# A two-layer graph kernel: the product with the values one slot later, with four buffers for the probabilities

## The chip, the cores and the metric

The kernel runs on one core of a Trainium2 chip. The metric is the device time of one execution in microseconds (us). A core has four engines that compute, each with its own instruction stream: TensorE (PE in the profile, with its weight loads shown apart as PEld), VectorE (DVE), ScalarE (ACT) and GpSimd (POOL). SyncE (SP) only starts DMAs here. The streams meet only through semaphores, and each engine runs its instructions in order.

## The reference

Two graph layers over 4096 nodes with a 4096 x 4096 adjacency matrix, each followed by a residual sum and a layer norm:

```
mask = adj > 0
agg  = mask @ x / max(rowsum(mask), 1)
h    = relu(concat(x @ W_self + b_self, agg @ W_nb + b_nb) @ W_comb + b_comb)
x    = layernorm(x + h)                                   # layer 0
xa   = tanh(x @ Wx1 + bx1) @ Wx2 + bx2                    # 32 wide
na   = tanh(neigh @ Wn1 + bn1) @ Wn2 + bn2
ws   = softmax(where(adj > 0, leaky_relu(xa @ na.T), -9e15))
out  = layernorm(x + concat(x @ Wfx + bfx, ws @ (neigh @ Wv + bv)))   # layer 1
```

## The kernel before

The rows of x are worked on in 32 blocks of 128. A block's 4096 columns are taken in 8 groups of 512, k = 0 to 7. All engines walk through the same list of slots; `due(s, AT, k)` says whether in slot s an engine has the work whose offset is AT: block b, group g where s - AT = 8b + g. Work written with k = 0 comes once in a block, in the slots that have the same remainder modulo 8; below, "remainder 0" means those slots. The number of a slot is an order and not a clock: an engine goes on to the next slot as soon as its semaphores let it.

A preparation makes fp16 pairs (high and low half) of x and of the neighbours' values, and the 32-wide attention vectors of the neighbours. `neigh_sb` holds the neighbours' rows for that; it is not read any more once the preparation is over. Then the blocks follow. In each slot:

- TensorE: `turn_p` (line 951, four transposes of exponentials into one of two banks `ps_t`), `aggregate` (lines 927 and 930, eight matmuls of the mask with x), once in a block some small steps of layer 0 and 1, then `scores` (line 942), and last `weigh_values` (line 964, twelve matmuls of the probabilities' halves with the values into `ps_v`).
- ScalarE: `exps` in every other slot (line 761), `p_high` (line 767, the high half of the probabilities from `ps_t`), `leaky` (line 754, scores out of `ps_s`). Once in a block `mean_of` (744), the copies 749 and 785, `x_tanh` (790), `xatt_high` (796), `normalise1` (773) and `normalise2` (779).
- VectorE: `masked_scores` (line 572, score plus bias, and a maximum), `make_mask` in every other slot (line 480), `p_low` last (line 618, the low half: `ps_t` minus the high half). Once in a block `row_scale` (624 to 628), `layer1` (636 to 642), `degrees` (587 and 590), `layer0` (596 to 603), `row_max`, and 608 and 613.
- GpSimd: `make_bias` in every other slot (line 408), `norm1`, `norm2` (398 to 402) and `add_biases` (393).
- SyncE: the transposing DMAs of the mask, the loads of adj, and once in a block a load of x and a store.

Transposes of group k are made in slot 30 + 8b + k and its product with the values, before the change, in slot 31 + 8b + k, behind the aggregation and the scores of that slot. `weigh_values` waits for `p_low` of its own group; `turn_p` of group k waits for `p_low` of group k - 2, since there are two banks; `p_high` of group k waits until the product of group k - 2 is done, since there are two buffers of halves. `layer1` reads `ps_v` when the block's last product is done, and the next block's first product waits for that.

In slots of remainder 0, `degrees` of a block is what `mean_of` waits for on ScalarE. Two slots later ScalarE makes `x_tanh` (line 790), and TensorE's `x_attention` (line 1008) waits for it behind the aggregation of its slot.

Of the kernel before, what the change touches and what calls it, by code (L numbers as in the profile page):

```python
# [5 lines left out]
F32, F16, BF16, F8 = mybir.dt.float32, mybir.dt.float16, mybir.dt.bfloat16, mybir.dt.float8e4  # L6
# [6 lines left out]
P = 128  # L13
N = 4096
D = 256
H = 32
DV = 128
# [6 lines left out]
NG = N // GW  # L24
# [14 lines left out]
NT = NB // TR  # L39
BIAS_BUFS = 3  # L40
RES_BUFS = 4

# [13 lines left out]
SCORE_AT = 20  # L58
ROW_MAX_AT = 28
TURN_AT = 30  # L60
WEIGH_AT = 31
LAYER1_AT = 39
SLOTS = NG * (NB - 1) + LAYER1_AT + 1


# [18 lines left out]
def at_least(eng, sem, value):  # L84
    if value > 0:
        eng.wait_ge(sem, value)


def gnn_kernel(nc, x, adj, w_self, b_self, w_nb, b_nb, w_comb, b_comb, neigh, wx1, bx1, wx2, bx2,
# [5 lines left out]
    with ExitStack() as ctx:  # L95
        def sb(name, shape, dt):
            return ctx.enter_context(nc.sbuf_tensor(name, shape, dt))

        def sem(name):
            return ctx.enter_context(nc.semaphore(name))  # L100

        x16 = sb("x16", [P, NC, XW], F16)
        neigh_sb = sb("neigh_sb", [P, NB, D], F32)
        m_both = sb("m_both", [P, DC, 2 * D], F32)
        v16 = sb("v16", [P, NC, 2 * DV], F16)
# [22 lines left out]
        mask_t8 = mask_t[:, :, :, :].rearrange("p a c n -> p (a c n)").bitcast(F8).rearrange(  # L128
            "p (a c n e) -> p a c e n", a=2, c=NC // 2, e=2)
        score = sb("score", [P, 2, N], F32)  # L130
        late = sb("late", [P, 2048], F32)
        p_both = late[:, 0:1024].bitcast(F16).rearrange("p (a b n) -> p a b n", a=2, b=2)
        p_hi, p_lo = p_both[:, 0], p_both[:, 1]
        res = late[:, 1024:2048].rearrange("p (r d) -> p r d", r=RES_BUFS)
        x_in = sb("x_in", [P, 2, D], F32)
        l0 = sb("l0", [P, D], F32)
        mean = sb("mean", [P, D], F32)
# [43 lines left out]
        ps_t = [ctx.enter_context(nc.psum_tensor(f"ps_t{k}", [P, GW], F32)) for k in range(2)]  # L181
        ps_v = ctx.enter_context(nc.psum_tensor("ps_v", [P, GW], F32))
# [53 lines left out]
        pv_done = sem("pv_done")  # L236
# [21 lines left out]
        p_hi_made = sem("p_hi_made")  # L258
# [99 lines left out]
        def _(pool):  # L358
# [31 lines left out]
            def add_biases(b):  # L390
                pool.wait_ge(x1_made, b + 1)
                at_least(pool, out_made, b - RES_BUFS + 1)
                pool.tensor_tensor(res[:, b % RES_BUFS, :], x1[:, :], bfv_sb[:, :], ALU.add).then_inc(resx_made, 1)  # L393

# [33 lines left out]
        def _(dve):  # L428
# [182 lines left out]
            def add_fx(b):  # L611
                dve.wait_ge(resx_made, b + 1)
                dve.tensor_tensor(res[:, b % RES_BUFS, 0:DV], ps_x[:, 3 * P:4 * P], res[:, b % RES_BUFS, 0:DV],
                                  ALU.add).then_inc(res_made, 1)

            def p_low(b, k):
                dve.wait_ge(p_hi_made, NG * b + k + 1)
                dve.tensor_tensor(p_lo[:, k % 2, :], ps_t[k % 2][:, :], p_hi[:, k % 2, :],  # L618
                                  ALU.subtract).then_inc(p_lo_made, 1)

            def row_scale(b):
# [46 lines left out]
        def _(act):  # L668
# [94 lines left out]

            def p_high(b, k):
                act.wait_ge(pt_done, NG * b + k + 1)
                at_least(act, pv_done, NG * b + k - 1)
                act.copy(p_hi[:, k % 2, :], ps_t[k % 2][:, :]).then_inc(p_hi_made, 1)  # L767

            def normalise1(b):
                act.wait_ge(norm1_step, 3 * (b + 1))  # L770
# [53 lines left out]
        def _(pe):  # L824
# [129 lines left out]
            def weigh_values(b, k):  # L954
                pe.wait_ge(p_lo_made, NG * b + k + 1)
                if k == 0:
                    at_least(pe, l1_step, 6 * (b - 1) + 4)
                    if b == 0:
                        pe.wait_ge(h_tanh, NT)
                for u in range(CG):  # L960
                    c = k * CG + u
                    chunk = slice(u * P, (u + 1) * P)
                    for part, (p, v) in enumerate(((p_hi, 0), (p_hi, DV), (p_lo, 0))):
                        mm = pe.matmul(ps_v[:, 0:DV], p[:, k % 2, chunk], v16[:, c, v:v + DV],  # L964
                                       start=(c == 0 and part == 0), stop=(c == NC - 1 and part == 2))
                mm.then_inc(pv_done, 1)

# [85 lines left out]
```

## Time and profile before

| what | value |
|---|---|
| median of 3 runs | 807.25 us (806.93 to 810.67) |
| the profiled execution | 808.58 us, of which span 806.8 us |
| PE busy | 766.1 us, 95% |
| DVE busy | 593.4 us, 74% |
| ACT busy | 560.9 us, 70% |
| POOL busy | 293.9 us, 36% |
| granted TensorE clock, mean | 0.981 |

The span is the time from the first to the last instruction. The first 100 us are the preparation and the first block, the loop runs to about 750 us, where the last block's aggregation ends, and the rest is the tail, in which only layer 1 of the last blocks is left. A "wait" in the profile is idle time of an engine just before an instruction, put down to what released it.

### The profile page before, as it was taken

What the parts mean: (1) busy time and instruction counts of PE and PEld (TensorE: products, weight loads), DVE (VectorE), ACT (ScalarE), POOL (GpSimd) and SP (SyncE); (2) the same over time, 40 slices, a digit from 0 to 9 for tenths busy, and PEclk for the clock granted to TensorE, in tenths of its full rate; (3) what the DMA queues carried; (4) which work ended last, traced back from release to release, by engine and by line L of the source; (5) the groups of instructions that cost most, each with busy time, mean ns of one, the idle gap of its engine ahead of it and who ended that gap; (6) DMA issues with size and microseconds to landing.
All of it is one profiled execution on the core that took longest, in us unless ns stands there. A gap on an engine that the chain in (4) does not pass through costs nothing.

```text
span 806.8 us, 20198 instructions
## 1 busy us (share of the span) xinstructions
PE 766.1 (95%) x7440; PEld 643.2 (80%) x7440; DVE 593.4 (74%) x1481; ACT 560.9 (70%) x1045; POOL 293.9 (36%) x368
## 2 busy tenths in 40 slices
PE   5679989999999999999999999999999999999885
PEld 4446666888888888888888888888888888888664
DVE  2667456878777777877877777777778777777784
ACT  2246236777777777787777777777777777777995
POOL 0004163443333334444444333333444444443101
PEclk9679999999999999999999999999999999999999
DMA  7905574445454554554445444455544544420000
GB/s 237 364 21 157 140 200 138 136 122 138 141 120 135 145 144 123 135 145 125 132 139 135 129 138 131 126 138 145 127 136 139 145 123 134 139 66 15 14 9 14
DMA packets 107403, 103.64 MB, mean 128 GB/s; under 512 B 74664, under 2 KB 88872, under 8 KB 107304
## 3 DMA queue, kind: packets, MB, share of 16 engines
q1 hardware_dynamic: 105872, 101.29, 45.1%
q8 instruction: 59, 0.97, 0.5%
q10 hardware_dynamic: 1432, 1.06, 0.4%
q14 instruction: 40, 0.33, 0.1%
HBM read 81.34 MB, written 4.19 MB: 106 GB/s over the span
## 4 chain that ended last, share of the span: by engine, by line
PE 87%; DVE 5%; ACT 2%; issue 2%; SPq 2%; DMA 1%; POOL 1%; POOLq 0%; ACTq 0%; DVEq 0%
PE ps_v L964 20%; PE ps_agg L930 13%; PE ps_agg L927 13%; PE ps_t L951 13%; PE ps_agg L982 7%; PE ps_s L942 7%; PE ps_x L1002 2%; PE ps_x L999 2%; SPq L328 2%; PE ps_x L1008 2%; PE ps_s L843 1%; PE ps_v L851 1%; PE ps_x L860 1%; DMA neigh_sb<-in_L_gnn_neigh_dram 1%; PE ps_agg L972 1%
## 5 line engine op out<-in xcount | busy, mean ns | idle before, releaser
L754 ACT ACTIVATE score<-ps_s,sc 128x512 f32<-128x512 f32 x256 | 177.8, 695 | 93.4 <-PE ps_s L942 89.5
L927 PE MATMUL ps_agg<-x,mask_t 128*128 128x257 f16 x1024 | 240.6, 273 | 0.0
L618 DVE TENSOR_TENSOR late<-ps_t,late 128x512 f16<-128x512 f32 x256 | 174.4, 681 | 85.3 <-ACT late L767 85.1
L930 PE MATMUL ps_agg<-x,mask_t 128*128 128x256 f16 x1024 | 235.4, 273 | 0.0
L572 DVE CUSTOM_DVE_ANT_0 score<-score,bias 128x512 f32<-128x512 f32 x256 | 191.1, 747 | 60.1 <-ACT score L754 59.9
L964 PEld LDWEIGHTS ps_v<-v,late 128*128 128x128 f16 x3072 | 191.7, 98 | 47.5 <-DVE late L618 13.7
L964 PE MATMUL ps_v<-v,late 128*128 128x128 f16 x3072 | 213.5, 219 | 7.6 <-DVE late L618 6.6
L767 ACT CAST late<-ps_t 128x512 f16<-128x512 f32 x256 | 147.8, 578 | 15.9 <-PE ps_t L951 15.6
L951 PE MATMUL ps_t<-ident,score 128*128 128x128 f32 x1024 | 155.7, 275 | 2.0 <-ACT score L761 1.8
L761 ACT ACTIVATE score<-score,exp_bias 128x1024 f32<-128x1024 f32 x128 | 146.5, 1145 | 0.8 <-DVE exp_bias L581 0.7
L408 POOL TENSOR_SCALAR bias<-mask 128x1024 bf16<-128x1024 uint8 x128 | 137.9, 1077 | 17.0 <-issue 6.3
L384 POOL TENSOR_SCALAR mv<-mv 128x1 f32<-128x1 f32 x32 | 8.5, 264 | 369.9 <-DVE mv L603 369.9
L930 PEld LDWEIGHTS ps_agg<-x,mask_t 128*128 128x128 fp8e4 x1024 | 99.7, 97 | 15.8 <-issue 4.9
L927 PEld LDWEIGHTS ps_agg<-x,mask_t 128*128 128x128 fp8e4 x1024 | 99.9, 98 | 14.8 <-issue 1.3
L951 PEld LDWEIGHTS ps_t<-ident,score 128*128 128x128 f32 x1024 | 107.8, 141 | 3.4 <-ACT score L761 3.2
L942 PE MATMUL ps_s<-n,stack 96*128 96x512 f16 x256 | 98.3, 384 | 0.0
L480 DVE TENSOR_SCALAR mask<-adj_sb 128x1024 uint8<-128x1024 int32 x128 | 89.7, 703 | 0.1
L982 PE MATMUL ps_agg<-m_both,mean_x_t 128*128 128x256 f32 x256 | 60.5, 379 | 0.0
L744 ACT ACTIVATE mean<-ps_agg,row 128x256 f32<-128x256 f32 x32 | 15.1, 473 | 59.7 <-DVE row L590 59.7
L982 PEld LDWEIGHTS ps_agg<-m_both,mean_x_t 128*128 128x128 f32 x256 | 46.1, 190 | 5.3
L398 POOL TENSOR_SCALAR mv<-mv 128x1 f32<-128x1 f32 x32 | 19.2, 601 | 49.0 <-DVE mv L642 49.0
L393 POOL TENSOR_TENSOR late<-x,bfv_sb 128x256 f32<-128x256 f32 x32 | 32.4, 1013 | 3.2 <-ACT x L773 0.7
(107 smaller groups left out, 739.9 us busy)
## 6 DMA issues: line engine op xcount, KB each, us to landing
adj_sb<-in_adj_dram SPq DMA_DIRECT2D x128, 512.0 KB, 4.0
neigh_sb<-in_L_gnn_neigh_dram SPq DMA_DIRECT2D x8, 512.0 KB, 13.6
score<-in_x_dram SPq DMA_DIRECT2D x8, 512.0 KB, 9.9
x_in<-in_x_dram SPq DMA_DIRECT2D x32, 128.0 KB, 3.7
out_dram<-out_sb SPq DMA_DIRECT2D x32, 128.0 KB, 3.9
mask_t<-mask SPq DMA_TRANSPOSE x128, 2.4
bias<-in_L_gnn_W_comb_dram ACTq DMA_DIRECT2D x1, 512.0 KB, 14.8
bias<-in_L_gnn_W_self_dram ACTq DMA_DIRECT2D x1, 256.0 KB, 8.2
```

What stands on the lines that cost most here:

```text
L408: pool.tensor_scalar(bias[:, b % BIAS_BUFS, part], mask[:, b % 2, part], BIG / EDGE, -BIG, ALU.mult, ALU.add).then_inc(bias_made, 1)
L572: dve.tensor_tensor_reduce(score[:, b % 2, part], score[:, b % 2, part], bias[:, b % BIAS_BUFS, part], 1.0, -3.0e38, ALU.add, ALU.max, par ...
L618: dve.tensor_tensor(p_lo[:, k % 2, :], ps_t[k % 2][:, :], p_hi[:, k % 2, :], ALU.subtract).then_inc(p_lo_made, 1)
L754: act.activation(score[:, b % 2, k * GW:(k + 1) * GW], ps_s[k % 2][:, :], ACT.Prelu, alpha=SLOPE, scale=score_scale).then_inc(leaky_made, 1)
L761: act.activation(part, part, ACT.Exp, bias=exp_bias[:, b % 2:b % 2 + 1], accum_out=sums[:, b % 2, q:q + 1]).then_inc(exp_made, 1)
L767: act.copy(p_hi[:, k % 2, :], ps_t[k % 2][:, :]).then_inc(p_hi_made, 1)
L927: mm = pe.matmul(agg[:, 0:D + 1], mask_t8[:, b % 2, c // 2, c % 2, :], x16[:, c, 0:D + 1], start=(c == 0), stop=(c == NC - 1), skip_group_ ...
L930: mm = pe.matmul(agg[:, 0:D], mask_t8[:, b % 2, c // 2, c % 2, :], x16[:, c, X_LO:X_LO + D], start=False, stop=False, skip_group_check=True)
L942: pe.matmul(ps_s[k % 2][:, :], stack[:, b % 2, :], n16[:, k * GW:(k + 1) * GW], start=True, stop=True).then_inc(s_done, 1)
L951: mm = pe.transpose(ps_t[k % 2][:, u * P:(u + 1) * P], score[:, b % 2, at:at + P], ident[:, :])
L964: mm = pe.matmul(ps_v[:, 0:DV], p[:, k % 2, chunk], v16[:, c, v:v + DV], start=(c == 0 and part == 0), stop=(c == NC - 1 and part == 2))
L982: mm = pe.matmul(ps_agg[b % 2][:, 0:D], mean_x_t[:, c * P:(c + 1) * P], m_both[:, dc, half * D:(half + 1) * D], start=(c == 0), stop=(c == ...
```

## The change

The two offsets `WEIGH_AT` and `LAYER1_AT` go up by one. So the product of a group comes two slots behind its transposes, and `row_scale`, `layer1`, `norm2`, `normalise2` and the store come one slot later. There are four buffers for the halves in place of two; they lie in the first 8 of the 32 row tiles of `neigh_sb`, and the residual rows `res` have a tile of their own. `p_high` of group k now waits for the product of group k - 4.

```diff
--- before.py
+++ after.py
@@ -39,6 +39,7 @@
 NT = NB // TR
 BIAS_BUFS = 3
 RES_BUFS = 4
+P_BUFS = 4
 
 
 
@@ -58,8 +59,8 @@
 SCORE_AT = 20
 ROW_MAX_AT = 28
 TURN_AT = 30
-WEIGH_AT = 31
-LAYER1_AT = 39
+WEIGH_AT = 32
+LAYER1_AT = 40
 SLOTS = NG * (NB - 1) + LAYER1_AT + 1
 
 
@@ -128,10 +129,11 @@
         mask_t8 = mask_t[:, :, :, :].rearrange("p a c n -> p (a c n)").bitcast(F8).rearrange(
             "p (a c n e) -> p a c e n", a=2, c=NC // 2, e=2)
         score = sb("score", [P, 2, N], F32)
-        late = sb("late", [P, 2048], F32)
-        p_both = late[:, 0:1024].bitcast(F16).rearrange("p (a b n) -> p a b n", a=2, b=2)
+        res = sb("res", [P, RES_BUFS, D], F32)
+
+        p_both = neigh_sb[:, 0:2 * P_BUFS, :].rearrange("p u n -> p (u n)").bitcast(F16).rearrange(
+            "p (b a n) -> p a b n", a=2, b=P_BUFS)
         p_hi, p_lo = p_both[:, 0], p_both[:, 1]
-        res = late[:, 1024:2048].rearrange("p (r d) -> p r d", r=RES_BUFS)
         x_in = sb("x_in", [P, 2, D], F32)
         l0 = sb("l0", [P, D], F32)
         mean = sb("mean", [P, D], F32)
@@ -615,7 +617,7 @@
 
             def p_low(b, k):
                 dve.wait_ge(p_hi_made, NG * b + k + 1)
-                dve.tensor_tensor(p_lo[:, k % 2, :], ps_t[k % 2][:, :], p_hi[:, k % 2, :],
+                dve.tensor_tensor(p_lo[:, k % P_BUFS, :], ps_t[k % 2][:, :], p_hi[:, k % P_BUFS, :],
                                   ALU.subtract).then_inc(p_lo_made, 1)
 
             def row_scale(b):
@@ -763,8 +765,8 @@
 
             def p_high(b, k):
                 act.wait_ge(pt_done, NG * b + k + 1)
-                at_least(act, pv_done, NG * b + k - 1)
-                act.copy(p_hi[:, k % 2, :], ps_t[k % 2][:, :]).then_inc(p_hi_made, 1)
+                at_least(act, pv_done, NG * b + k - P_BUFS + 1)
+                act.copy(p_hi[:, k % P_BUFS, :], ps_t[k % 2][:, :]).then_inc(p_hi_made, 1)
 
             def normalise1(b):
                 act.wait_ge(norm1_step, 3 * (b + 1))
@@ -961,7 +963,7 @@
                     c = k * CG + u
                     chunk = slice(u * P, (u + 1) * P)
                     for part, (p, v) in enumerate(((p_hi, 0), (p_hi, DV), (p_lo, 0))):
-                        mm = pe.matmul(ps_v[:, 0:DV], p[:, k % 2, chunk], v16[:, c, v:v + DV],
+                        mm = pe.matmul(ps_v[:, 0:DV], p[:, k % P_BUFS, chunk], v16[:, c, v:v + DV],
                                        start=(c == 0 and part == 0), stop=(c == NC - 1 and part == 2))
                 mm.then_inc(pv_done, 1)
```

Lines behind the new constant stand one number higher, and two numbers higher from the tile of `res` on (964 is 966).

On VectorE the change moves `row_scale` and `layer1` relative to the other work. Before, between the score masking of remainder 6 and the end of remainder 7 (`late` holds the halves and the residual rows, L618 is `p_low`):

```order
L624 TENSOR_REDUCE row<-sums 128x1
L626 RECIPROCAL row<-row 128x1
L628 TENSOR_SCALAR row<-row,sc 128x1
L618 TENSOR_TENSOR late<-ps_t,late 128x512
L636 SCALAR_TENSOR_TENSOR late<-ps_v,row,late 128x128
L639 BN_STATS stat<-late 128x6
L642 BN_AGGR mv<-stat 128x2
L572 ISA score,part_max<-score,bias 128x512
L572 ISA part_max 128x1
L480 TENSOR_SCALAR mask<-adj_sb 128x1024
L618 TENSOR_TENSOR late<-ps_t,late 128x512
```

After it, from `p_low` of remainder 6 to `degrees` (L589) of remainder 0:

```order
L620 TENSOR_TENSOR neigh_sb<-ps_t,neigh_sb 128x512
L574 ISA score,part_max<-score,bias 128x512
L574 ISA part_max 128x1
L626 TENSOR_REDUCE row<-sums 128x1
L628 RECIPROCAL row<-row 128x1
L630 TENSOR_SCALAR row<-row,sc 128x1
L482 TENSOR_SCALAR mask<-adj_sb 128x1024
L620 TENSOR_TENSOR neigh_sb<-ps_t,neigh_sb 128x512
L638 SCALAR_TENSOR_TENSOR res<-ps_v,row,res 128x128
L641 BN_STATS stat<-res 128x6
L644 BN_AGGR mv<-stat 128x2
L574 ISA score,part_max<-score,bias 128x512
```

`row_scale` went from ahead of `p_low` of remainder 6 to behind the score masking of remainder 7, and `layer1` from ahead of that masking to ahead of the masking of remainder 0, so that it now stands between the mask conversion and `degrees`.

On ScalarE `normalise2` moves. Before, from the scores of remainder 0 to the tanh of remainder 2:

```order
L754 ACTIVATE score<-ps_s,sc 128x512
L779 ACTIVATE out_sb<-late,mv 128x256
L761 ACTIVATE score,sums<-score,exp_bias 128x1024
L767 CAST late<-ps_t 128x512
L754 ACTIVATE score<-ps_s,sc 128x512
L749 COPY mean_x_t<-ps_agg 128x512
L790 ACTIVATE tanh_sb<-ps_x,bx_sb 32x128
```

And after it, the same stretch:

```order
L756 ACTIVATE score<-ps_s,sc 128x512
L763 ACTIVATE score,sums<-score,exp_bias 128x1024
L769 CAST neigh_sb<-ps_t 128x512
L756 ACTIVATE score<-ps_s,sc 128x512
L781 ACTIVATE out_sb<-res,mv 128x256
L751 COPY mean_x_t<-ps_agg 128x512
L792 ACTIVATE tanh_sb<-ps_x,bx_sb 32x128
```

The same seven instructions stand there, with `normalise2` behind the second `leaky` instead of behind the first.

## Rows read from the trace of the kernel before

**Rows 1.** Stretch, its length, busy us of PE, PEld, DVE, ACT, POOL, clock, DMA.

```profile
400.00:600.00 200.00, 200.00 (x2059) 173.60 (x2059) 155.96 (x403) 151.25 (x288) 81.90 (x100) 1.00 0.50 134
```

**Rows 2.** Waits: us in total, times, longest; whole span, then 760 us to the end.

```profile
PE ps_v L964 <- DVE late L618: 6.6, 14, 1.3
...
PE ps_v L964 <- DVE late L618: 4.7, 12, 0.7
```

**Rows 3.** Line 1008, 160 to 740 us: ns, first and last start; then idle before it.

```profile
L1008 PEld LDWEIGHTS ps_x<-tanh_sb,wx_sb x54: 154/156/158, 164.1 to 729.6; 32*96 32x96 f32 x54
...
  ACT tanh_sb L790: 5.7, 27
```

**Rows 4.** Timeline, TensorE, line 1008: start us, us, what, [idle before <-releaser].

```profile
105.13 0.24 PEld L1008 LDWEIGHTS ps_x<-tanh_sb,wx_sb 32*96 32x96 f32 x2 [0.21 <-issue]
...
425.08 0.24 PEld L1008 LDWEIGHTS ps_x<-tanh_sb,wx_sb 32*96 32x96 f32 x2 [0.21 <-ACT tanh_sb L790]
...
750.35 0.46 PE L1008 MATMUL ps_x<-tanh_sb,wx_sb 32*96 32x128 f32 x2 [1.09 <-ACT tanh_sb L790]
```

**Rows 5.** Timeline, ScalarE, three places of the loop and one near the end.

```profile
414.72 0.69 ACT L754 ACTIVATE score<-ps_s,sc 128x512 f32<-128x512 f32 x1 [0.40 <-PE ps_s L942]
...
419.75 0.47 ACT L744 ACTIVATE mean<-ps_agg,row 128x256 f32<-128x256 f32 x1 [1.92 <-DVE row L590]
...
424.57 0.35 ACT L790 ACTIVATE tanh_sb<-ps_x,bx_sb 32x128 f32<-32x128 f32 x1
...
425.90 0.69 ACT L754 ACTIVATE score<-ps_s,sc 128x512 f32<-128x512 f32 x1 [0.52 <-PE ps_s L942]
...
749.94 0.35 ACT L790 ACTIVATE tanh_sb<-ps_x,bx_sb 32x128 f32<-32x128 f32 x1
```

**Rows 6.** Timeline, VectorE, 413 to 427 us.

```profile
413.68 1.19 DVE L572 CUSTOM_DVE_ANT_0 score<-score,bias 128x512 f32<-128x512 f32 x1
...
414.81 0.14 DVE L624 TENSOR_REDUCE row<-sums 128x1 f32<-128x4 f32 x1
...
415.91 0.34 DVE L636 SCALAR_TENSOR_TENSOR late<-ps_v,row,late 128x128 f32<-128x128 f32 x1
...
416.87 0.69 DVE L572 CUSTOM_DVE_ANT_0 score<-score,bias 128x512 f32<-128x512 f32 x1
...
417.49 0.70 DVE L480 TENSOR_SCALAR mask<-adj_sb 128x1024 uint8<-128x1024 int32 x1
418.11 0.67 DVE L618 TENSOR_TENSOR late<-ps_t,late 128x512 f16<-128x512 f32 x1
418.70 0.67 DVE L572 CUSTOM_DVE_ANT_0 score<-score,bias 128x512 f32<-128x512 f32 x1
...
419.31 0.21 DVE L587 TENSOR_SCALAR row<-ps_agg,sc 128x1 f32<-128x1 f32 x1
...
426.62 0.69 DVE L572 CUSTOM_DVE_ANT_0 score<-score,bias 128x512 f32<-128x512 f32 x1 [0.51 <-ACT score L754]
```

**Rows 7.** Chain of waits, 400 to 425 us, a piece on line 964: start us, us.

```profile
417.11 0.67 PE ps_v L964 x12
```

**Rows 8.** Timeline, GpSimd, 413 to 417 us.

```profile
413.30 1.04 POOL L408 TENSOR_SCALAR bias<-mask 128x1024 bf16<-128x1024 uint8 x1
...
415.55 1.04 POOL L408 TENSOR_SCALAR bias<-mask 128x1024 bf16<-128x1024 uint8 x1
```

**Rows 9.** Timeline near the start of the block loop, VectorE and GpSimd.

```profile
113.42 1.23 DVE L572 CUSTOM_DVE_ANT_0 score<-score,bias 128x512 f32<-128x512 f32 x1 [1.36 <-ACT score L754]
...
114.19 1.37 POOL L408 TENSOR_SCALAR bias<-mask 128x1024 bf16<-128x1024 uint8 x1
...
114.59 1.52 DVE L480 TENSOR_SCALAR mask<-adj_sb 128x1024 uint8<-128x1024 int32 x1
116.03 1.51 DVE L572 CUSTOM_DVE_ANT_0 score<-score,bias 128x512 f32<-128x512 f32 x1
```

**Rows 10.** Chain of waits, after 785 us, a piece on line 964.

```profile
797.99 0.84 PE ps_v L964 x12
```

## The prediction, written before the kernel ran

> **What bounds the kernel now.** I read the busy time by stretch first. From 400 to 600 us TensorE is busy for 200.00 of 200.00 us at clock 1.00, VectorE for 155.96 and ScalarE for 151.25 [rows 1]. So between the start and the tail only TensorE's own work counts, or something that makes it wait. Next the waits of the products with the values, which the change is about: over the whole span TensorE waits 6.6 us for `p_low`, and 4.7 of these lie behind 760 us [rows 2]. The loop has none of them to give. Third, I asked of each TensorE step that the loop holds up how near its releaser comes. One is close: line 1008, which the profile says waited 5.7 us in 27 places for the tanh; those 27 start 21.75 us apart ((729.6 - 0.1 - 164.1) / 26, the last start being the second of its pair), which is the time of a block [rows 3]. The gap before it is 0.21 us, but it was also 0.21 us at 105 us, where the profile names no releaser [rows 4]; so the gap belongs to the instruction. In the tail, where it truly waited, it began 0.06 us behind the end of the tanh (749.94 + 0.35 = 750.29, start 750.35) [rows 4, 5]. In the loop the tanh ends at 424.57 + 0.35 = 424.92, is seen at 424.98, and line 1008 begins at 425.08 [rows 4, 5]. The tanh is 0.10 us early: that is all the slack there is, once in each block.
>
> **Part 1: later products, four buffers.** The instructions are the same in number, shape and duration; only addresses differ, and those I cost at nothing (bounds: 0, since the new tiles are read and written by the same engines with the same patterns). In the loop the wait that is relaxed does not exist, so it gives 0. Where the loop ends, one group of twelve products less has been done under TensorE's bound, and moves to the tail, where there is room: such a group is 0.67 us of the chain [rows 7]. I take -0.7. In the tail the chain of waits passes through such a group in front of a transpose four times after 785 us, the last of them at 797.99 [rows 10]; with one slot more between them the transposes go first, and wait only for their bank. The bounds are one group of 0.67, so 0.7, and four, 2.7; I take 1.7, the middle, since ScalarE's exponentials, which stay on the chain, set the pace where they stand. The last product still waits for its own `p_low`.
>
> **Part 2: row_scale and layer1 on VectorE.** They are what can touch the loop, since `degrees`, for which ScalarE waits 1.92 us in each block [rows 5], comes behind them. I walk through one block with the durations of before.
>
> - The masking at 413.68 is unchanged; the next instruction starts at 414.81 [rows 6]. That is now `p_low`, which takes 0.59 from start to next start (418.11 to 418.70) [rows 6], so VectorE is free at 415.40.
> - The masking of remainder 7 waits for `leaky` at 414.72. With such a wait the masking starts 0.72 behind it (425.90, 426.62) [rows 5, 6]: 415.44, against 416.87 before.
> - This is the point. GpSimd's `make_bias` starts at 415.55 [rows 8], and these two get in each other's way. The masking at 413.68 took 1.19 instead of 0.69: it started while the one of 413.30 was running, to 414.34, and the next instruction came 0.47 later [rows 6, 8]. So did the mask conversion at 114.59, which took 1.52 instead of 0.70: `make_bias` of 114.19 ended at 115.56, and 116.03 is 0.47 later [rows 6, 9]. That `make_bias` took 1.37 instead of 1.04, held by the masking that ended at 114.65: it ended 1.04 after 114.52, so a masking lets go 0.13 before its end [rows 9].
> - Applied here: the masking of 415.44 is first, ends at 416.13 and lets go at 416.00; `make_bias` runs to 417.04. VectorE goes on at 415.44 + 0.61 = 416.05, `row_scale` takes 0.51 (0.59 of `p_low` off 415.91 - 414.81) [rows 6], and the mask conversion stands at 416.56 with `make_bias` in front of it. What follows it starts at 417.04 + 0.47 = 417.51.
> - `p_low` to 418.10. `layer1` needs the block's last product, which ends at 417.11 + 0.67 = 417.78 [rows 7], so it does not wait; it takes 0.96 (416.87 - 415.91) [rows 6], to 419.06. The masking takes 0.61 (418.70 to 419.31) [rows 6], and `degrees` starts at 419.67 against 419.31: 0.36 us late.
>
> From `mean_of` to the tanh ScalarE runs without a gap, 4.82 us (419.75 to 424.57) [rows 5]. After the change the same ten instructions stand there, `normalise2` among them, only in another order, so the delay of 0.36 goes through whole. 0.10 of it is slack, and TensorE waits 0.26 us at line 1008. What comes behind shifts with TensorE, since ScalarE is ahead again in the next slots (it waits for the scores at 425.90 [rows 5]), so each block pays once. The 27 places of [rows 3] are the blocks in which this happens: 27 x 0.26 = +7.0 us. If the two engines did not hold each other up, the walk would be: conversion at 416.56 plus 0.62 (417.49 to 418.11) [rows 6], `p_low` to 417.77, `layer1` from 417.84 (0.06 behind the product), `degrees` at 417.84 + 0.96 + 0.61 = 419.41, 0.10 late. `leaky` of the next slot would then meet its own wait for the scores, since `normalise2` no longer fills the time ahead of it; I estimate 0.07 of wait per block, +1.9 us.
>
> The Trainium skill ("SBUF — State Buffer", section "Who interferes with whom") says that VectorE and GpSimd take a shared port pair as an exclusive lock for a whole instruction, and that the one that starts first decides who blocks. The rows at 114 us agree (1.52 against 0.70 us); by that rule the sum has +7.0, without it +1.9.
>
> **The rest.** `norm2` moves with `layer1`: GpSimd is idle there and `normalise2` is needed 4 us later, so it costs 0. The mask conversion of remainder 1 may come about 1 us late behind the moved `make_bias`; its DMA is used five slots later. The first product of a block waits for the first instruction of `layer1` (418.10 + 0.34), and comes in TensorE a slot behind the product of 417.11, so some 2 us later, since a block's 21.75 us hold eight slots. SyncE's order is unchanged. No wait is added anywhere. All of this is 0, and behind 0.7 us more delay it still would be.
>
> **Sum.** 7.0 - 0.7 - 1.7 = +4.6 us. On the profiled execution's 808.58 us that is 813.2; that execution lies 1.3 above the median of 807.25, and I set the prediction against the median: 811.9 us.
>
> **Rivals.**
> - *The engines hardly meet* (the 0.10 delay, with +1.9): 807.25 + 1.9 - 2.4 = 806.8. For it: the masking and `make_bias` start only 0.11 us apart, and both `make_bias` rows of the loop took 1.04 us, held by nothing [rows 8]; the case that I need, held and holding in turn, is seen only near the start [rows 9]. Against it: the masking was held in every block.
> - *GpSimd is first* (slower, much). If the masking starts behind 415.55, it waits for `make_bias` to end at 416.59, the next instruction starts at 417.06, `row_scale` to 417.57, the conversion is free to 418.19, `p_low` to 418.78, `layer1` to 419.74, `degrees` at 420.35: 1.04 late, 0.94 on TensorE, 27 x 0.94 = +25.4, less 2.4: 830.2. It decides from 0.11 us of delay in `leaky`, or an earlier GpSimd. The Trainium skill ("Perfetto Trace Analysis", section "GPSIMD Engine Instruction") warns that GpSimd's spans in a profile are unreliable; the spacings here repeat to 0.01 us, but the true moment at which the port is taken may lie off the shown start.
> - *The waits for p_low were worth all that they show*, and the loop pays nothing: 6.6 + 0.7 = 7.3 us off, 800.0. For it: the chain of the tail runs through them. Against it: 4.7 of them lie where ScalarE's exponentials take over as soon as TensorE no longer waits.
> - *The change does nothing*, the wait for `p_low` coming back at `turn_p` two slots later, with no stall in the loop: 807.25.
>
> **How the numbers follow.** Forecast 0.54, engines hardly meet 0.22, GpSimd first 0.08, all waits gone 0.09, nothing 0.07. The bound for a difference is 0.5%, 4.0 us: 811.3 and 803.2. The forecast's +4.6 lies near that bound; with 0.05 us of error in a block (1.4 us) and 1 us in the tail, I give 0.7 of it to slower and 0.3 to the same. Slower: 0.38 + 0.08 = 0.46. Faster: 0.09 and a little of the second, 0.11. Same: 0.43. The range leaves out GpSimd first (0.08) and most of all waits gone: 804.0 to 815.5, from the tail's better bound with no stall to the forecast with 0.4 us in each block. The forecast's own range is 809 to 815.
>
> **What would show it.** Right: idle time before line 1010 (now) of about 0.47 us per block (0.21 + 0.26) with the tanh as its releaser; a block period of 22.0 instead of 21.75 us; mask conversions of about 1.1 us in remainder 7; `degrees` about 0.36 us later against the scores of its slot; `make_bias` of about 1.5 us once per block. The tail, from the last aggregation to the end, shorter by about 2.4 us. Wrong: a period that stays at 21.75 us, or one near 22.7; or a tail that keeps its length.

## The result and the profile after

The changed kernel takes 815.19 us in the median of 4 runs (812.42 to 817.33), against 807.40 us (806.93 to 810.67, 4 runs); the ratio is 1.0088, with a 95% interval of 1.0052 to 1.0125. Run again later, beside other kernels, it took 814.26 us, a ratio of 1.0084 (1.0063 to 1.0105). So it is slower by 0.8 to 0.9%. The time is 3.3 us above the predicted 811.9 and lies in the stated range of 804.0 to 815.5, but only 0.3 us below its upper end.

The profiled execution took 812.42 us, with a span of 810.6 us. The busy time by stretch that answers to [rows 1], with the columns of there:

```profile
400.00:600.00 200.00, 198.34 (x2036) 171.67 (x2034) 164.75 (x400) 149.56 (x283) 84.39 (x101) 1.00 0.48 132
```

TensorE, which was busy for all of the 200 us, now stands for 1.66 us of them. VectorE is busy for 9 us more, with fewer instructions: the 37 mask conversions took 25.4 us before and 36.7 us now. Most of that is the conversion of remainder 1, which now takes 1.52 us (one starts at 423.18) and holds TensorE up nowhere: tanh_ahead, below, has the same 36.7 us and a period of 21.75 us. The changed line 1008, now 1010, answers to [rows 3]:

```profile
L1010 PEld LDWEIGHTS ps_x<-tanh_sb,wx_sb x54: 154/156/158, 161.8 to 734.2; 32*96 32x96 f32 x54
...
  ACT tanh_sb L792: 17.6, 54
```

The 27 blocks now start (734.2 - 0.1 - 161.8) / 26 = 22.01 us apart instead of 21.75. This distance is what tells the loss. The 17.6 us of idle time count both the weight load (0.46 us each time) and the matmul behind it, which now waits too (about 0.19 us, nine times in the 200 us above); and 0.21 us of each gap were there before. The next rows show one block of the changed kernel on VectorE, for [rows 6]:

```profile
414.27 1.19 DVE L574 CUSTOM_DVE_ANT_0 score<-score,bias 128x512 f32<-128x512 f32 x1
...
416.03 0.69 DVE L574 CUSTOM_DVE_ANT_0 score<-score,bias 128x512 f32<-128x512 f32 x1
...
417.16 1.01 DVE L482 TENSOR_SCALAR mask<-adj_sb 128x1024 uint8<-128x1024 int32 x1
418.09 0.67 DVE L620 TENSOR_TENSOR neigh_sb<-ps_t,neigh_sb 128x512 f16<-128x512 f32 x1
418.69 0.33 DVE L638 SCALAR_TENSOR_TENSOR res<-ps_v,row,res 128x128 f32<-128x128 f32 x1
...
419.64 0.69 DVE L574 CUSTOM_DVE_ANT_0 score<-score,bias 128x512 f32<-128x512 f32 x1
...
420.26 0.21 DVE L589 TENSOR_SCALAR row<-ps_agg,sc 128x1 f32<-128x1 f32 x1
```

Its GpSimd, for [rows 8]:

```profile
416.14 1.49 POOL L410 TENSOR_SCALAR bias<-mask 128x1024 bf16<-128x1024 uint8 x1
```

And ScalarE and the weight load of line 1010, for [rows 5] and [rows 4]:

```profile
420.70 0.47 ACT L746 ACTIVATE mean<-ps_agg,row 128x256 f32<-128x256 f32 x1 [2.27 <-DVE row L592]
...
425.52 0.35 ACT L792 ACTIVATE tanh_sb<-ps_x,bx_sb 32x128 f32<-32x128 f32 x1
...
425.93 0.24 PEld L1010 LDWEIGHTS ps_x<-tanh_sb,wx_sb 32*96 32x96 f32 x2 [0.46 <-ACT tanh_sb L792]
```

This block lies 0.59 us later in its trace than the one of before (414.27 against 413.68). With that taken off, the masking starts at 415.44, the mask conversion at 416.57, `degrees` at 419.67, against 419.31 before: 0.36 us late. From the mean to the tanh it is 4.82 us as before. The tanh ends at 425.87, and line 1010 begins 0.06 us behind it, with a gap of 0.46 us instead of 0.21. The masking of 416.03 came 0.11 us ahead of `make_bias`, which took 1.49 us and held the conversion (1.01 us instead of 0.70).

The end of the program is another matter. The last block's masking of remainder 7, on VectorE, and the `make_bias` beside it:

```profile
746.18 1.18 DVE L574 CUSTOM_DVE_ANT_0 score<-score,bias 128x512 f32<-128x512 f32 x1 [0.46 <-ACT score L756]
...
750.14 0.21 DVE L589 TENSOR_SCALAR row<-ps_agg,sc 128x1 f32<-128x1 f32 x1
```

```profile
745.78 1.05 POOL L410 TENSOR_SCALAR bias<-mask 128x1024 bf16<-128x1024 uint8 x1
```

Here GpSimd was first by 0.40 us, and the masking took 1.18. `degrees` of the last block starts 3.00 us behind the last aggregation matmul (747.14), against 2.08 before (744.68 behind 742.60). From that matmul to the first exponentials of the last block the changed kernel takes 44.63 us and the kernel before 43.88; from these exponentials to the end of the last instruction shown, which issues the store, it is 17.00 against 18.43. It looks as if GpSimd made `degrees` late here. But `layer1` waits for the last product of its block. Here are that product and the first instruction of `layer1`, in the changed kernel and then, with the masking ahead of them, in bias_cut (an experiment below, in which this `make_bias` is made small):

```profile
747.69 0.83 PE L966 MATMUL ps_v<-v,neigh_sb 128*128 128x128 f16 x12
...
748.56 0.35 DVE L638 SCALAR_TENSOR_TENSOR res<-ps_v,row,res 128x128 f32<-128x128 f32 x1
```

```profile
743.39 0.69 DVE L574 CUSTOM_DVE_ANT_0 score<-score,bias 128x512 f32<-128x512 f32 x1 [0.47 <-ACT score L756]
...
744.90 0.83 PE L966 MATMUL ps_v<-v,neigh_sb 128*128 128x128 f16 x12
...
745.77 0.35 DVE L638 SCALAR_TENSOR_TENSOR res<-ps_v,row,res 128x128 f32<-128x128 f32 x1
```

`layer1` starts 0.04 us behind the product's end in both. In bias_cut the masking is free (0.69 us), and `degrees` still starts 3.00 us behind the last aggregation matmul (747.35 behind 744.35). So in the last block VectorE waits for the product whether GpSimd holds it up or not; what makes `degrees` late is `layer1`, which stands behind that product and in front of `degrees`.

The changed tail's chain of waits, behind 797 us (start us, us):

```profile
797.08 0.83 PE ps_v L966 x12
...
798.36 0.67 PE ps_v L966 x12
...
799.47 0.67 PE ps_v L966 x12
...
800.58 0.67 PE ps_v L966 x12
...
801.94 0.67 PE ps_v L966 x12
...
804.55 0.86 PE ps_v L966 x12
```

The products are still on the chain [rows 10]. They now alternate with the transposes without a wait for `p_low`, until the last one.

One table for all the kernels below that kept the loop: from the traces, in us, the start of `x_attention` of the first block, from there to that of the fourth block, the period of the loop, and from the last `x_attention` of the loop (the thirtieth block's) to the end of the span.

| kernel | first x_attention | to the fourth | period | to the end |
|---|---|---|---|---|
| before | 105.13 | 58.99 | 21.75 | 77.3 |
| changed | 102.52 | 59.29 | 22.01 | 76.5 |
| changed, again | 105.54 | 58.36 | 22.01 | 76.6 |
| degrees_ahead | 105.51 | 56.63 | 21.82 | 75.9 |
| row_scale_early | 105.28 | 59.39 | 22.18 | 76.5 |
| bias_cut | 105.00 | 58.96 | 21.82 | 76.5 |
| tanh_ahead | 104.67 | 60.23 | 21.75 | 76.0 |
| four_buffers_only | 104.18 | 59.06 | 21.75 | 77.3 |
| both_ahead | 105.58 | 56.07 | 21.75 | 75.4 |
| before_both_ahead | 103.78 | 56.19 | 21.75 | 75.9 |
| before_degrees_ahead | 103.78 | 56.66 | 21.75 | 76.4 |
| degrees_first | 104.77 | 56.07 | 21.75 | 74.6 |

The first column differs by up to 3 us between executions of kernels with the same preparation. So spans of single executions are compared from the second column on. The second column needs care too, because TensorE's clock fell in the second block of some of these executions and not of others. The first row is of the changed kernel, and the second, 3 us later, of the same place when it was run again (stretch, its length, busy us of PE, PEld, DVE, ACT, POOL, clock, DMA):

```profile
117.00:120.00 3.00, 3.00 (x14) 2.11 (x13) 1.63 (x5) 1.36 (x3) 0.00 (x0) 0.51 0.45 138
```

```profile
120.00:123.00 3.00, 2.38 (x17) 1.67 (x17) 1.70 (x5) 1.41 (x3) 0.00 (x0) 1.00 0.44 131
```

At 0.50 the clock is at 1.2 GHz, at 1.00 at 2.4 GHz. Ahead of both TensorE had stood for 2.95 and 2.94 us for the mean. The kernel is the same and so is the wait, but up to the fourth block one execution takes 59.29 us and the other 58.36: the low stretch cost 0.93 us. The kernel before had such a stretch as well (0.51 from 120 to 123 us), and so had four_buffers_only, row_scale_early and bias_cut; in tanh_ahead it was about twice as long (60.23 us in the table). None of the five kernels with `degrees` ahead of the masking had one (1.00 from 117 to 126 us). From 165 to 740 us the clock is 1.00 in the kernel before and in the changed one.

### The profile page after: what moved, and what is told of

Read it like the earlier page. It is cut to its first block, busy times and chain, and to the rows that moved or that the text cites. A ratio compares the mean times of both kernels' runs of the same rounds, so it can differ in the third digit from the quotient of the medians.

```text
span 810.6 us, 20196 instructions
## 1 busy us (share of the span) xinstructions
PE 765.9 (94%) x7440; PEld 644.3 (79%) x7440; DVE 624.2 (77%) x1481; ACT 561.0 (69%) x1045; POOL 295.3 (36%) x368
## 4 chain that ended last, share of the span: by engine, by line
DVE 31%; PE 31%; ACT 18%; issue 15%; SPq 2%; DMA 1%; POOL 1%; ACTq 0%; POOLq 0%; DVEq 0%
DVE score L574 9%; DVE neigh_sb L620 7%; PE ps_agg L984 7%; ACT score L756 5%; ACT score L763 4%; PE ps_v L966 4%; PE ps_agg L932 3%; PE ps_agg L929 3%; ACT neigh_sb L769 3%; PE ps_t L953 3%; PE ps_s L944 2%; DVE mask L482 2%; ACT mean_x_t L751 2%; PE ps_x L1010 2%; DVE stat L603 2%
## 5 line engine op out<-in xcount | busy, mean ns | idle before, releaser
L966 PEld LDWEIGHTS ps_v<-v,neigh_sb 128*128 128x128 f16 x3072 | 193.0, 98 | 38.4 <-DVE neigh_sb L620 3.4
L620 DVE TENSOR_TENSOR neigh_sb<-ps_t,neigh_sb 128x512 f16<-128x512 f32 x256 | 173.9, 679 | 63.1 <-ACT neigh_sb L769 62.7
L966 PE MATMUL ps_v<-v,neigh_sb 128*128 128x128 f16 x3072 | 213.2, 219 | 2.3 <-DVE res L638 2.3
L410 POOL TENSOR_SCALAR bias<-mask 128x1024 bf16<-128x1024 uint8 x128 | 162.8, 1272 | 16.6 <-issue 5.9
L769 ACT CAST neigh_sb<-ps_t 128x512 f16<-128x512 f32 x256 | 148.4, 580 | 14.3 <-PE ps_t L953 14.3
L482 DVE TENSOR_SCALAR mask<-adj_sb 128x1024 uint8<-128x1024 int32 x128 | 120.9, 947 | 0.1
L395 POOL TENSOR_TENSOR res<-x,bfv_sb 128x256 f32<-128x256 f32 x32 | 32.4, 1012 | 3.2 <-ACT x L775 0.7
```

What stands on the lines that cost most here:

```text
L410: pool.tensor_scalar(bias[:, b % BIAS_BUFS, part], mask[:, b % 2, part], BIG / EDGE, -BIG, ALU.mult, ALU.add).then_inc(bias_made, 1)
L482: dve.tensor_scalar(mask[:, b % 2, q * QW:(q + 1) * QW], adj_sb[:, q, :], 0.0, float(EDGE), ALU.is_gt, ALU.mult).then_inc(mask_made, 1)
L620: dve.tensor_tensor(p_lo[:, k % P_BUFS, :], ps_t[k % 2][:, :], p_hi[:, k % P_BUFS, :], ALU.subtract).then_inc(p_lo_made, 1)
L769: act.copy(p_hi[:, k % P_BUFS, :], ps_t[k % 2][:, :]).then_inc(p_hi_made, 1)
L966: mm = pe.matmul(ps_v[:, 0:DV], p[:, k % P_BUFS, chunk], v16[:, c, v:v + DV], start=(c == 0 and part == 0), stop=(c == NC - 1 and part == 2))
```

## The experiments

**degrees_ahead.** The changed kernel, with `degrees` moved up within its slot on VectorE:

```diff
+                if d := due(s, MEAN_AT, 0):
+                    degrees(d[0])
                 if d := due(s, SCORE_AT + 1):
                     masked_scores(*d)
...
-                if d := due(s, MEAN_AT, 0):
-                    degrees(d[0])
```

> The changed kernel with `degrees` ahead of the score masking in its slot on VectorE, the rest as changed. Theory (late `degrees` makes the tanh late, and TensorE waits for it at `x_attention`): the masking's 0.61 us go from in front of `degrees`, which then comes 0.25 us earlier than in the kernel before; period of a block back to 21.75 us, gap before `x_attention` back to 0.21 us, 7.0 us off the changed kernel in the loop and some 0.6 more at the last block. Against the kernel before it keeps the shorter tail: 1 to 2 us faster. Rival (the loop lost its time to the later product or to the other tiles): the period stays at 22.01 us and the time at that of the changed kernel.

Measured: 806.35 us against 807.87, ratio 0.9975 (0.9963 to 0.9987). So the slot order of one small step turns the change from 0.8% slower to 0.25% faster; the rival falls. The period, though, is 21.82 and not 21.75. ScalarE shows why (this kernel's timeline, from the mean to the tanh):

```profile
418.29 0.47 ACT L746 ACTIVATE mean<-ps_agg,row 128x256 f32<-128x256 f32 x1 [1.63 <-DVE row L592]
...
422.03 0.69 ACT L756 ACTIVATE score<-ps_s,sc 128x512 f32<-128x512 f32 x1 [0.32 <-PE ps_s L944]
422.62 0.59 ACT L781 ACTIVATE out_sb<-res,mv 128x256 f32<-128x256 f32 x1
423.11 0.57 ACT L751 COPY mean_x_t<-ps_agg 128x512 f32<-128x512 f32 x1
423.57 0.35 ACT L792 ACTIVATE tanh_sb<-ps_x,bx_sb 32x128 f32<-32x128 f32 x1
```

ScalarE is early enough now to wait for the scores of its slot, and `normalise2`, which the change put behind these scores, and the copy stand between them and the tanh: 423.57 - 422.03 = 1.54 us. The mean is no longer what makes the tanh late, but by these rows the move of `normalise2` still costs 0.07 us per block; no run moved `normalise2` alone. The prediction had this 0.07, for the case without holding up; the expectation here had lost it.

**row_scale_early.** The changed kernel, with `row_scale` where it was before the change:

```diff
-                if d := due(s, LAYER1_AT - 1, 0):
+                if d := due(s, LAYER1_AT - 2, 0):
                     row_scale(d[0])
```

> The changed kernel with `row_scale` back in the slot in which it was before, remainder 6, ahead of `p_low`. Theory (who is first at the masking of remainder 7, VectorE or `make_bias`, sets how long VectorE stands): the masking now starts 0.36 us behind `make_bias` and waits for its end, the mask conversion is free, and `degrees` comes 0.53 us later than in the kernel before in place of 0.36: period 22.18 us, +4.6 us on the changed kernel. Rival (no holding up between the two engines; only the place of `layer1` counts): VectorE waits for the product either way, `degrees` is 0.10 us late, period 21.82 us.

Measured: 819.53 us in one run, period 22.18 us. VectorE, and then GpSimd, in remainder 7 of one block:

```profile
421.17 1.22 DVE L574 CUSTOM_DVE_ANT_0 score<-score,bias 128x512 f32<-128x512 f32 x1
...
422.32 0.68 DVE L482 TENSOR_SCALAR mask<-adj_sb 128x1024 uint8<-128x1024 int32 x1
```

```profile
420.80 1.04 POOL L410 TENSOR_SCALAR bias<-mask 128x1024 bf16<-128x1024 uint8 x1
```

Now the masking is 0.37 us behind `make_bias`, is held (1.22 us), `make_bias` is not (1.04), and the conversion is free (0.68). The one who starts first decides who waits. The forecast period came out to 0.01 us.

**bias_cut.** The changed kernel, with one `make_bias` of four made small:

```diff
-                part = slice(q * QW, (q + 1) * QW)
+                part = slice(q * QW, q * QW + (64 if b >= 3 and q == 2 else QW))
```

> The changed kernel, in which the `make_bias` of remainder 7 (third quarter of the columns) writes only 64 of its 1024 columns from the fourth block on; the other columns keep older values. Theory (that `make_bias` holds up the mask conversion): the conversion takes 0.70 us again instead of 1.01, `degrees` comes 0.26 us earlier than in the changed kernel, and the period is 21.75 to 21.82 us. Rival (the conversion is slow for another reason, or `degrees` is late for another one): 1.01 us and 22.01 us as they are.

Measured: 809.62 us in one run, period 21.82 us. VectorE and GpSimd:

```profile
416.09 0.69 DVE L574 CUSTOM_DVE_ANT_0 score<-score,bias 128x512 f32<-128x512 f32 x1
...
417.22 0.69 DVE L482 TENSOR_SCALAR mask<-adj_sb 128x1024 uint8<-128x1024 int32 x1
```

```profile
416.19 0.69 POOL L410 TENSOR_SCALAR bias<-mask 128x64 bf16<-128x64 uint8 x1
```

The conversion is back at 0.69 us, and 0.19 of the 0.26 us per block are gone; the small `make_bias` itself was held for most of its 0.69 us by the masking ahead of it (in the last block, where nothing held it, it took 0.24 us). So the holding up makes 0.19 us, and the remaining 0.07 has the cause read at degrees_ahead.

**changed_again.** No edit.

> The changed kernel as it is, once more. Theory: period 22.01 us in 27 blocks, tail as before; its runs lay from 812.4 to 817.3 us, and the part ahead of the loop, in which the inputs are loaded, holds the spread: with the first `x_attention` at 102.5 us in the first profile, a slower execution should show it later, and the rest of the span unchanged. Rival (the loop itself varies): other periods in a slower execution.

Measured: 814.26 us, 813.22 to 817.07. In its profiled execution (span 812.8 us, against 810.6 in the first) the period is 22.01 us again, and the first `x_attention` comes at 105.54 instead of 102.52 us; up to the fourth block 0.93 us of these 3.02 is made up, which is the low clock stretch that the first profile had there and this one had not. The part ahead of the loop holds the difference between these two. An execution near 817 us was not profiled, but the mean granted clock of every execution is on record, and the spread goes with it. The changed kernel's executions of 817.05, 817.33 and 817.07 us had 0.980; those of 812.42, 813.33, 813.22, 813.68 and 813.97 us had 0.987. Beside this run the kernel before took 807.7 us in the median of its seven executions at 0.987, and the changed kernel 813.7 us in its three: 6.0 us more. In the profiles the clock is below 1.00 in two places of the preparation (24 to 40 and 52 to 64 us in the changed kernel, 0.68 and 0.72), in the second block, and at the end when TensorE is done. Which of these places makes 817 out of 813 us stays open.

**tanh_ahead.** The changed kernel, with the tanh and the copy exchanged on ScalarE; `degrees` stays late:

```diff
-                if d := due(s, MEAN_COPY_AT, 0):
-                    mean_x_t_copy(d[0])
...
                 if d := due(s, XATT_AT, 0):
                     x_tanh(d[0])
+                if d := due(s, MEAN_COPY_AT, 0):
+                    mean_x_t_copy(d[0])
```

> The changed kernel with the tanh ahead of the copy of the transposed means in its slot on ScalarE. `degrees` stays as late as it is. Theory (the tanh is the only thing in the loop that is late): it comes 0.47 us earlier, period 21.75 us, -6.8 us in the loop. Rival (something else would be late next, by `degrees` or by the copy): the period stays above 21.75 us.

Measured: 808.35 us in one run, period 21.75 us. The whole loss of the loop goes away, as forecast, while `degrees` is as late as in the changed kernel (3.00 us behind the last aggregation). The tanh was the only thing in the loop that came too late.

**four_buffers_only.** The new tiles without the later product:

```diff
-WEIGH_AT = 32
-LAYER1_AT = 40
+WEIGH_AT = 31
+LAYER1_AT = 39
```

> Four buffers in the neighbours' rows and the tile of its own for the residual rows, but the product one slot behind and `layer1` where it was before. Theory (the buffers and their place cost and give nothing): period 21.75 us, time of the kernel before within 0.5 us. Rival (the other tiles cost something): longer operations on the halves, a period above 21.75 us.

Measured: 807.46 against 807.67 us, ratio 0.9993 (0.9980 to 1.0006). The tiles and the number of buffers cost and give nothing.

**two_buffers.** The later product without the buffers:

```diff
-P_BUFS = 4
+P_BUFS = 2
```

> The changed kernel with two buffers for the halves in place of four. The high half of group k then waits for the product of group k - 2, which stands last in the same slot. Theory: in remainder 1 the cast starts only behind the product, about 0.25 us later than it does now, with the scores, `normalise2`, the copy and the tanh behind it: period about 22.25 us, +6 us on the changed kernel, and the tail longer, since transposes, cast and product go one after another. Rival (four buffers are not needed for the later product): 22.01 us and the same tail.

Measured: 898.28 us, period 24.46 us. The direction was right and the size wrong by far: 84 us instead of 6. The waits of this kernel from 400 to 600 us (us, times, longest):

```profile
ACT neigh_sb L769 <- PE ps_v L966: 43.0, 41, 1.9
...
PE ps_x L1010 <- ACT tanh_sb L792: 9.6, 8, 1.2
...
PE ps_v L966 <- DVE res L638: 3.8, 8, 0.5
```

I had moved only the cast of remainder 1. In fact the cast waits for a product in five slots of eight, so ScalarE stands 43 us in 200; `p_low` and with it `layer1`, the first product of the next block and `degrees` get late. The waits show that these are late, not how much each adds to the next. Retiming one instruction holds as long as the queues behind it are idle for longer than the delay; here they were not.

**both_ahead** and **before_both_ahead.** The two moves together, by the edits shown under degrees_ahead and tanh_ahead, on the changed kernel and on the kernel before.

> The changed kernel with `degrees` ahead of the score masking and the tanh ahead of the copy of the means. With `degrees` ahead alone the period was 21.82 us, since the tanh then stands behind the second scores, `normalise2` and the copy. Theory: with the copy behind it as well the period is 21.75 us, 1.9 us less in the loop than with `degrees` ahead alone, and the time some 3 us (0.4%) below the kernel before: 1.4 from the tail behind the last block's first exponentials, 0.4 to 0.7 from the product that moves out of the loop, the rest from the last block's earlier `degrees`. Rival (21.82 us has another cause): the period stays, and the time at that of `degrees` ahead alone.

> The kernel before with the same two moves and nothing of the change. Theory: its loop has no wait that they could take away, period 21.75 us; only the last block's earlier `degrees` shows, up to 0.6 us less. So it stays within 0.1% of the kernel before, and what the version with the change and both moves gains beyond it is what the later product is worth, some 2 us. Rival (the gain comes from the two moves alone, and the later product is worth nothing): both kernels end at the same time.

Measured: 803.40 us, ratio 0.9934 (0.9918 to 0.9949), with the change; 804.04 us, ratio 0.9944 (0.9929 to 0.9959), without it. The first came as forecast, with a period of 21.75 us and more gain. For the second the theory fails: it gains 4 us where at most 0.6 was expected, and the rival is nearly right. The gain is not in the loop: both take 2.8 to 2.9 us less than the kernel before up to the fourth block, and with the two moves on the kernel before the stretch to the end is 1.3 us shorter. TensorE at the second block's transposes of the mean, before and in before_degrees_ahead:

```profile
118.44 0.44 PE L972 MATMUL ps_agg<-ident,mean 128*128 128x128 f32 x2 [2.93 <-ACT mean L744]
```

```profile
115.64 0.44 PE L972 MATMUL ps_agg<-ident,mean 128*128 128x128 f32 x2 [1.48 <-ACT mean L744]
```

The masking in front of `degrees` took 1.51 us there [rows 9], held by `make_bias`; with `degrees` ahead of it TensorE waits 1.45 us less. Another 0.9 us is the clock: in the kernel before it was 0.51 from 120 to 123 us, and in both kernels here it stayed at 1.00. That the shorter wait keeps it up fits all profiles but one: changed_again waited 2.94 us and kept it as well. So the link between the move and the clock is likely and not shown.

**degrees_first** and **before_degrees_ahead.** The first is both_ahead with `degrees` ahead of `layer1` as well (the edit below is against both_ahead); the second is the kernel before with `degrees` ahead of the masking alone.

```diff
+                if d := due(s, MEAN_AT, 0):
+                    degrees(d[0])
                 if d := due(s, LAYER1_AT, 0):
                     layer1(d[0])
-                if d := due(s, MEAN_AT, 0):
-                    degrees(d[0])
```

> The changed kernel with the tanh ahead of the copy, and `degrees` ahead of `layer1` too, as the first thing of its slot on VectorE. Theory (the tail of the changed kernel starts late because `layer1`, 0.96 us, stands in front of the last `degrees`): from the last aggregation matmul to the first exponentials of the last block it takes about 42.6 us in place of 43.5, and from there to the end 17.0 as in the changed kernel; the loop's period stays at 21.75 us, since the product of remainder 0 is some 0.7 us behind the first instruction of `layer1` and `degrees` takes 0.45. Time 0.9 us below the version with both moves. Rival (that stretch is longer for the later product itself): 43.5 us and the same time.

> The kernel before with `degrees` ahead of the score masking and nothing else. Theory, formed after both moves took 4 us off the kernel before: the gain is all `degrees`, at two places that are not the loop, the second block (TensorE waited 2.93 us for the mean there, and 1.49 with both moves) and the last one; the tanh's place gives nothing. Time as with both moves, about 0.995 of the kernel before. Rival (the tanh's place carries part of it, in the second block, where TensorE also stood at `x_attention`): less than 3 us of gain.

Measured: degrees_first takes 802.40 us, ratio 0.9922 (0.9900 to 0.9943), the fastest kernel here. From the last aggregation matmul to the last block's first exponentials it takes 42.67 us, against 43.47 in both_ahead, and from there to the end 17.01. The theory holds: the late `degrees`, not the later product in itself, made that stretch long. Where `degrees` starts 1.25 us behind the last aggregation matmul the stretch is 42.67 us with the later product and 42.58 without it (before_both_ahead). before_degrees_ahead takes 804.37 us, ratio 0.9942 (0.9920 to 0.9964). Between its first `x_attention` and the end it is 3.2 us shorter than before, and before_both_ahead 4.1 us; so `degrees` gives three quarters (of its 3.2 us, 1.4 are the wait in the second block, 0.9 the clock there and 0.9 lie behind the loop), and the tanh's place, which I had put at nothing, about 1 us, half in the second block and half behind the loop.

What the later product itself is worth is the difference between degrees_first and before_both_ahead, both without a late `degrees` and with a period of 21.75 us: 0.1 us up to the fourth block and 1.35 us behind the loop, 1.5 us or 0.2% by the traces. The intervals of the two ratios overlap, so the runs alone do not tell them apart.

## Why the prediction was right

The mechanism of the loop was right and carries the result. Two smaller terms were mis-sized, both in the same direction, and the median then came out just inside the range (and 0.2 us outside the forecast's own 809 to 815) partly by the mixture of clocks among four executions. One of the prediction's own signs, a tail shorter by about 2.4 us, did not come: it is 0.7 us shorter.

- *The loop has no wait for `p_low` to give.* Right: with the buffers alone nothing changed, and with the later product and both moves the loop is at 21.75 us, as before.
- *`degrees` 0.36 us late, 0.26 us per block at line 1008, 27 times.* Right to the hundredth: 419.67, a period of 22.01 us, and 26 periods and the one ahead of them give 7.1 us against 7.0. Four experiments bear on the cause: take the holding up away (bias_cut) and 0.07 stays, turn round who is first (row_scale_early) and 0.43 comes, take the masking from in front of `degrees` and 0.07 stays, give the tanh room and nothing stays.
- *0.07 without holding up.* Right: it came out in degrees_ahead and in bias_cut. The rows put it down to the place of `normalise2`, and it went away when the tanh no longer stood behind the copy; no run moved `normalise2` alone.
- *-0.7 where one group of products leaves the loop.* Mis-sized: it gave 0.1. The block with that slot is 0.40 to 0.48 us shorter in the two profiles of the changed kernel (19.54 and 19.46 against 19.94 us between the second and the third `x_attention`), but the low clock of the kernel before lasted beyond its second `x_attention` (122.44; the clock was 0.50 from 122 to 123 and 0.75 from 123 to 124 us), so its 19.94 is too long. With the clock at 1.00 in both, the block takes 19.37 us with the later product (both_ahead) and 19.49 without it (before_both_ahead). The second block's 17.73 and 16.89 us in the two profiles of the changed kernel differ by the clock too.
- *-1.7 in the tail.* Mis-sized. The piece from the last block's exponentials to the end gave 1.43, inside the bounds of 0.7 and 2.7. What the sum left out is the stretch ahead of it, 0.75 us longer: there the last block has no mask conversions, VectorE reaches `layer1` before the product that `layer1` needs, and `degrees` behind it came 0.92 us late. The tail gave 0.7. GpSimd was first at the masking there, as in the rival "GpSimd is first", but it is not the cause: in bias_cut the masking was free and `degrees` just as late, and only moving `degrees` ahead of `layer1` (degrees_first) took the whole delay away.
- *The sum.* From the first `x_attention` to the end the changed kernel takes 6.4 us more than before in the first pair of profiles and 5.6 in the second, against +4.6. With the sizes measured the prediction's sum is 7.1 - 0.1 - 0.7 = 6.3. The medians differ by 7.8 and 6.4 us, and by 6.0 among executions with the same mean clock of 0.987. The 7.8 is high by chance: two of the four executions of the changed kernel had 0.980 and took 817 us.
- *The rivals.* Engines hardly meet, all waits gone, and nothing: refuted by the period. Their weight of 0.38 came from a walk whose one decisive margin was 0.11 us; the margin held in the loop, where the period is 22.01 us in both profiles of the changed kernel. "GpSimd is first" at its forecast price is refuted too, since the period would have been 22.7 us.

## What to carry to other kernels

When an engine is busy for the whole of a loop, moving a step pays nothing there and can only cost: look for the step with the least slack among those that the busy engine waits for (here 0.10 us, ahead of a 32-row matmul), and ask which of the moved instructions now stands in front of it on the other engines. A small step that opens a chain for the bounding engine should stand first in its slot; moving `degrees` ahead of one masking gave the kernel before 3.2 us by the traces, twice what the later product gives; 0.9 of it is TensorE's clock, which did not fall in the second block. So when two single profiles are compared, the granted clock is read stretch by stretch first. And where two engines share a resource, retime both: an order changed on one of them decides who is first in a place that the change never names.

## What the runs showed that I had not expected

- The holding up between VectorE and GpSimd is as regular as the instructions themselves: a masking or a mask conversion that starts while `make_bias` runs goes on when it ends, and the next instruction starts 0.46 to 0.48 us behind that end, in the kernel before, in the changed one and with the order turned round.
- `make_bias` on 64 columns instead of 1024 took 0.69 us behind a masking that had started 0.10 us earlier, and 0.24 us in bias_cut's last block, where nothing held it; the other 0.45 is waiting.
- With two buffers instead of four a wait that I had put at 0.25 us per block grew to 2.7 us per block (24.46 against 21.75), with five casts of eight waiting for a product.
